# The attention's weighing of values as three fp32r products, its low parts on VectorE and GpSimd, with five places for x and a new order at the end of the attention

## What is computed

```
x = x + tanh(g_xattn) * (softmax(mask(q k^T / sqrt(512))) v Wo^T + bo)   # q, k, v: linear in layernorm(x), ctx, ctx
scores = layernorm(x) gate_w^T; probs = softmax(scores)                  # n, t, e
g, m = top_k(probs over the tokens, k = 2 * 2048 / 8)
h = gelu(x[m] w1[e]) w2[e]                                               # x here: layernorm(x)
x = x + tanh(g_ffn) * scatter_add(g * h at m)
```

## Time and profile before

| | us |
|---|---|
| median of 3 runs | 1527.88 (1527.38 to 1529.64) |
| the profiled execution | 1530.52 |
| its span, first to last instruction | 1528.8 |
| TensorE busy | 1490.4 (97%) |
| VectorE, ScalarE, GpSimd busy | 991.0, 737.8, 557.4 |
| attention: first weighing, last weighing ends | 56.65, 153.86 |

### The profile page before, as it was taken

The page is one execution under the profiler, slowest core; times in us unless marked ns, Lnnn a source line. Parts: engine busy times, 40 slices in busy tenths (PEclk is TensorE's granted clock), DMA queues, the critical chain, the costliest instruction groups (busy, mean ns, idle before and its releaser), DMA issues.

```text
span 1528.8 us, 20345 instructions
## 1 busy us (share of the span) xinstructions
PE 1490.4 (97%) x7329; PEld 1227.4 (80%) x7329; DVE 991.0 (65%) x1737; ACT 737.8 (48%) x1298; POOL 557.4 (36%) x527
## 2 busy tenths in 40 slices
PE   7988899999999999999999999999999999999997
PEld 7765677888888888888888888888888888888886
DVE  3678875568757675767567666766667665766543
ACT  2267543455445544454445444545445545554533
POOL 2253344635443244404432344314440444323311
PEclk9999999999999999999999999999999999999999
DMA  7285623624324433334324423342424332442133
GB/s 234 79 281 173 205 91 111 172 83 104 105 89 84 110 99 95 76 92 106 93 90 90 116 85 110 70 120 67 131 51 114 85 111 83 83 111 83 42 77 76
DMA packets 101386, 163.37 MB, mean 107 GB/s; under 512 B 7411, under 2 KB 45315, under 8 KB 101285
## 3 DMA queue, kind: packets, MB, share of 16 engines
q1 hardware_dynamic: 86672, 128.16, 26.7%
q0 software_dynamic: 14400, 33.56, 11.5%
q10 hardware_dynamic: 213, 0.34, 0.1%
HBM read 128.48 MB, written 33.55 MB: 106 GB/s over the span
## 4 chain that ended last, share of the span: by engine, by line
PE 91%; DVE 4%; DMA 2%; ACT 2%; issue 1%; POOL 1%; POOLq 0%; SPq 0%; DVEq 0%; ACTq 0%
PE bank L1511 43%; PE bank L1397 35%; PE bank L1373 5%; PE bank L1690 2%; PE bank L601 1%; PE bank L577 1%; PE bank L418 1%; DMA x_s<-in_x 1%; PE bank L566 1%; DVE x L902 1%; ACT xn L656 0%; DVE atleast L1070 0%; PE bank L412 0%; DMA raw_k<-in_L_xattn_Wk 0%; PE bank L1560 0%
## 5 line engine op out<-in xcount | busy, mean ns | idle before, releaser
L1511 PE MATMUL bank<-w2hl,hh 128*128 128x512 f32 x2024 | 628.4, 392 | 0.5 <-DVE hid_low L1489 0.5
L1397 PE MATMUL bank<-xo,whl 128*128 128x512 f32 x2352 | 541.6, 389 | 0.1
L1397 PEld LDWEIGHTS bank<-xo,whl 128*128 128x128 f32 x2352 | 441.3, 188 | 92.3 <-issue 0.4
L1511 PEld LDWEIGHTS bank<-w2hl,hh 128*128 128x128 f32 x2024 | 375.9, 188 | 75.6 <-DVE hid_low L1489 0.9
L1511 PE MATMUL bank<-w2hl,hid_low 128*128 128x512 f32 x1012 | 394.0, 389 | 0.0
L1511 PEld LDWEIGHTS bank<-w2hl,hid_low 128*128 128x128 f32 x1012 | 190.0, 188 | 39.6
L1637 POOL DMA_INDIRECT layer_out<-y,slot_row x64 | 104.3, 1629 | 295.6 <-ACT y L1550 280.3
L1356 DVE TENSOR_TENSOR w2hl<-raw,w2hl 128x512 fp32r<-128x512 f32 x215 | 150.5, 722 | 41.3 <-ACT w2hl L1351 41.3
L1325 POOL TENSOR_TENSOR whl<-raw,whl 128x512 fp32r<-128x512 f32 x56 | 81.3, 1451 | 258.3 <-ACT whl L1282 258.3
L1351 ACT ACTIVATE w2hl<-raw 128x512 fp32r<-128x512 f32 x228 | 136.5, 624 | 64.5 <-DMA raw<-in_L_ffn_w 43.3
L1330 POOL TENSOR_TENSOR whl<-wsum,whl 128x512 fp32r<-128x512 f32 x56 | 73.0, 1303 | 183.5 <-ACT whl L1303 183.5
(11 more groups left out here) (243 smaller groups left out, 1747.4 us busy)
## 6 DMA issues: line engine op xcount, KB each, us to landing
raw<-in_L_ffn_w SPq DMA_DIRECT2D x228, 256.0 KB, 2.7
raw<-in_L_ffn_w SPq DMA_DIRECT2D x72, 512.0 KB, 4.9
x_s<-in_x SPq DMA_DIRECT2D x8, 1024.0 KB, 9.6
layer_out<-x SPq DMA_DIRECT2D x8, 1024.0 KB, 10.1
xn_rows<-xn SPq DMA_DIRECT2D x8, 1024.0 KB, 5.2
raw_k<-in_L_xattn_Wk SPq DMA_DIRECT2D x1, 1024.0 KB, 6.5
raw_q<-in_L_xattn_Wq SPq DMA_DIRECT2D x1, 1024.0 KB, 8.7
raw_v<-in_L_xattn_Wv SPq DMA_DIRECT2D x1, 1024.0 KB, 11.1
```

The lines of the kernel that those rows point to most:

```text
L1397: last = pe.matmul(bk[:, :], whl[:, p % 2, part, 2 * w + k, :], xo[:, xpart, x, k, :], start=(not adds and k == 0 and part == HIGH and xpa ...
L1511: last = pe.matmul(Y_BANKS[c][:, :], high if hpart == HIGH else low[:, c * P:(c + 1) * P], w2hl[:, f % 4, part, :], start=(s == 0 and hpar ...
```

## The change

- All quads but the last are weighed by three fp32r products (`weigh_pe`). `vo` is split in high and low once, in prep: high copies by ScalarE (batch 0) and VectorE (batch 1) from PSUM ahead of the copies of before, low parts by GpSimd. The turned exponentials are split for each quad: ScalarE makes the high part from `eT` after its copy (`e_high`); the low part (`weights_low`) is made by VectorE in quads 0 to 3, between `router_in` and `weights_in`, and by GpSimd in quads 4 to 6, between the mask biases and the deviations.
- In quads 0 to 3 two of the x transposes go between the weighings.
- x has five places, two of them where raw_v and raw_o were; quads 3 and 4 are loaded in prep as these are turned, later ones when the quad five back is added. `square` and `weigh` read the same tiles there.
- Quad 3: only its first two tiles are squared by ScalarE; VectorE takes the other two with its statistics (`late_half`), after the softmax step of quad 4.
- Quad 6: `router_in` goes ahead of `values_dve`. Quad 7: ScalarE's copies of w1 go behind the exponentials and their copy.
- After the quads the tokens' low parts go ahead of the w1 halves (one of which stood between weighings) and of both last `logits_out`; the two w2 low parts go behind `choice_start_dve` of batch 1. ScalarE alternates tokens and squares.

The diff, without the new tensors' and semaphores' lines and `x_tile`, which picks a quad's place:

```diff
@@ -160,8 +161,10 @@
             raw_v, raw_o, wvT, woT = (outward.enter_context(nc.sbuf_tensor(n, [P, KD, D], F32))
                                       for n in ("raw_v", "raw_o", "wvT", "woT"))
         with ExitStack() as there:
-            there.enter_context(nc.sbuf_tensor("front", [P, 2, KD, CAP], F32R))
+            x_far = there.enter_context(nc.sbuf_tensor("x_far", [P, 2, Q, D], F32))
             spare = there.enter_context(nc.sbuf_tensor("spare", [P, 2, Q, D], BF16))
+            vo_split = there.enter_context(nc.sbuf_tensor("vo_split", [P, 2, D], F32R))
+            eT_split = there.enter_context(nc.sbuf_tensor("eT_split", [P, 2, Q * P], F32R))
         xp = overlay("xp", [P, B, 2, KD, CAP], F32R)
         hid1 = overlay("hid1", [P, KF, CAP], F32)
         hid1_low = keep("hid1_low", [P, KF, CAP], F32R)
@@ -527,6 +542,10 @@
                                                  gates[:, 0:1], ALU.add, ALU.mult)
                 elif name == "vo":
                     eng.wait_ge(consts, 3)
+                    if i == 0:
+                        eng.activation(vo_split[0:J, HIGH, :], bk[0:J, :], ACT.Copy).then_inc(vo_high, 1)
+                    else:
+                        eng.tensor_copy(vo_split_1[0:J, HIGH, :], bk[0:J, :]).then_inc(vo_high_1, 1)
                     last = copy(vo[0:J, i, :], bk[0:J, :])
                 elif name == "vg":
                     last = copy(vg[0:J, :, 0:E], bk[0:J, 0:B * E].rearrange("p (b e) -> p b e", b=B))
@@ -598,6 +619,19 @@
         def weigh_pe(pe, q, i):
             n = Q * q + i
             wait(pe, added, n - 1)
+            if q < SPLIT_QUADS:
+
+                if i == 0:
+                    pe.wait_ge(vo_low, q // QB + 1)
+                    pe.wait_ge(e_high, q + 1)
+                for epart, part in ((HIGH, HIGH), (HIGH, LOW), (LOW, HIGH)):
+                    if i == 0 and epart == LOW:
+                        pe.wait_ge(e_low, q + 1)
+                    last = pe.matmul(O_BANKS[n % 2][:, :], eT_split[0:J, epart, i * P:(i + 1) * P],
+                                     (vo_split, vo_split_1)[q // QB][0:J, part, :], start=(epart == HIGH and part == HIGH),
+                                     stop=(epart == LOW))
+                last.then_inc(weighed, 1)
+                return
             pe.matmul(O_BANKS[n % 2][:, :], eT[:, q % 2, i * P:(i + 1) * P], vo[:, q // QB, :],
                       start=True, stop=True).then_inc(weighed, 1)
@@ -630,11 +664,16 @@
                 for i in range(2):
                     weigh_pe(pe, q, i)
                 between(q, 1)
-                weigh_pe(pe, q, 2)
-                between(q, 2)
-                weigh_pe(pe, q, Q - 1)
-                between(q, 3)
-                for i in range(Q):
+                if q < QB:
+                    for i in range(2):
+                        turn_x(pe, q + 2, i)
+                        weigh_pe(pe, q, i + 2)
+                else:
+                    weigh_pe(pe, q, 2)
+                    between(q, 2)
+                    weigh_pe(pe, q, Q - 1)
+                    between(q, 3)
+                for i in range(2 if q < QB else 0, Q):
                     if q + 2 < NQ:
                         turn_x(pe, q + 2, i)
                     if i == 1:
@@ -647,6 +686,12 @@
             for c in range(NC):
                 tokens_pe(pe, 0, c)
+        def weights_low(eng, q):
+
+            eng.wait_ge(e_high, q + 1)
+            eng.tensor_tensor(eT_split[0:J, LOW, :], eT[0:J, q % 2, :], eT_split[0:J, HIGH, :].bitcast(F32),
+                              ALU.subtract).then_inc(e_low, 1)
+
         def rows_act(act, q, tiles):
             for i in tiles:
@@ -677,7 +722,7 @@
                     act.wait_ge(x1_mean, q - LATE + 2)
                 ins = act.activation(spare[:, 1, i, :], x1[:, q % 2, i, :], ACT.Square,
                                      bias=x1mean[:, q % 2, i:i + 1], accum_out=x1var[:, q % 2, i:i + 1])
-                if i == Q - 1:
+                if i == (Q // 2 if q == LATE else Q) - 1:
                     ins.then_inc(x1_squares, 1)
             def x_out(q, i):
@@ -700,25 +745,21 @@
                     act.wait_ge(weighed, Q * (q - 1))
                 act.wait_ge(consts, 3)
                 act.activation(eT[0:J, q % 2, :], turn_bank(("e", q, 0))[0:J, :], ACT.Copy).then_inc(turn_out, 1)
+                if q < SPLIT_QUADS:
+                    wait(act, weighed, Q * q)
+                    act.wait_ge(turn_out, turn_at["e", q, 0] + 1)
+                    act.activation(eT_split[0:J, HIGH, :], eT[0:J, q % 2, :], ACT.Copy).then_inc(e_high, 1)
             for q in range(2):
                 for i in range(Q):
                     x_out(q, i)
             prep_out(act, prep_act, True, 1)
             for q in range(NQ):
-                if q == NQ - 1:
-                    for p in range(2):
-                        w1_high_act(act, 0, 0, p)
-                elif q - 1 >= LATE:
+                if LATE <= q - 1 < NQ - 2:
                     for i in range(Q // 2):
                         square_x1(q - 1, i)
                 exps(q)
-                if q == CHOOSE_FROM:
-
-                    for i in range(Q // 2, Q):
-                        square_x1(q - 1, i)
-                    e_out(q)
-                elif CHOOSE_FROM < q < NQ - 1:
+                if CHOOSE_FROM < q < NQ - 1:
                     square_x1(q - 1, Q // 2)
                     e_out(q)
                     square_x1(q - 1, Q - 1)
@@ -727,6 +768,8 @@
                 if q == CHOOSE_FROM:
                     choice_act(act, 0)
                 if q == NQ - 1:
+                    for p in range(2):
+                        w1_high_act(act, 0, 0, p)
                     for f in range(2):
                         w2_high_act(act, 0, 0, f)
                     for i in range(Q):
@@ -742,11 +785,10 @@
             for i in range(2):
                 square_x1(NQ - 1, i)
-            first_tokens_act(act, 0)
-            for i in range(2, Q):
-                square_x1(NQ - 1, i)
-            for c in range(1, NC):
+            for c in range(NC):
                 first_tokens_act(act, c)
+                if c < 2:
+                    square_x1(NQ - 1, c + 2)
         def attention_pool(pool):
             own = Tally(pool_own)
@@ -771,7 +813,12 @@
                     own.mark(pool.tensor_scalar(nm[:, s, 0, :], mv[:, s, :, 1], EPS, None, ALU.add))
                     own.mark(pool.tensor_scalar(nm[:, s, 1, :], mv[:, s, :, 0], -1.0, None, ALU.mult))
                 else:
-                    own.mark(pool.tensor_scalar(nm[:, s, 0, :], x1var[:, s, :], 1.0 / D, EPS, ALU.mult, ALU.add))
+                    tiles = Q // 2 if q == LATE else Q
+                    own.mark(pool.tensor_scalar(nm[:, s, 0, 0:tiles], x1var[:, s, 0:tiles], 1.0 / D, EPS, ALU.mult,
+                                                ALU.add))
+                    if q == LATE:
+                        pool.wait_ge(late_stats, 1)
+                        own.mark(pool.tensor_scalar(nm[:, s, 0, tiles:Q], mv[:, s, tiles:Q, 1], EPS, None, ALU.add))
                 pool.wait_ge(pool_own, own.n)
                 pool.tensor_tensor(nm[:, s, 2, :], nm[:, s, 0, :], powers[:, :], ALU.pow).then_inc(deviated2, 1)
                 pool.wait_ge(deviated2, q + 1)
@@ -820,6 +867,16 @@
                 mask_biases(it + 1)
                 if it == 0:
                     first_deviations(1)
+                    pool.wait_ge(vo_high, 1)
+                    wait_evacuated(pool, step_at["vo", 0])
+                    pool.tensor_tensor(vo_split[0:J, LOW, :], vo[0:J, 0, :], vo_split[0:J, HIGH, :].bitcast(F32),
+                                       ALU.subtract).then_inc(vo_low, 1)
+                    pool.wait_ge(vo_high_1, 1)
+                    wait_evacuated(pool, step_at["vo", 1])
+                    pool.tensor_tensor(vo_split_1[0:J, LOW, :], vo[0:J, 1, :], vo_split_1[0:J, HIGH, :].bitcast(F32),
+                                       ALU.subtract).then_inc(vo_low, 1)
+                if QB <= it < SPLIT_QUADS:
+                    weights_low(pool, it)
                 q = it - 1
                 if q >= 0:
                     deviations(q)
@@ -918,6 +975,17 @@
                     last = dve.bn_aggr(mv2[:, q % 2, i, :], st2[:, i, :])
                     own.mark(last) if i < Q - 1 else last.then_inc(x1_stats, 1)
+            def late_half():
+
+                dve.wait_ge(x1_stats, LATE)
+                dve.wait_ge(deviated2, LATE - 1)
+                for i in range(Q // 2, Q):
+                    own.mark(dve.bn_stats(st2[:, i, :], x1[:, LATE % 2, i, :]))
+                dve.wait_ge(dve_own, own.n)
+                for i in range(Q // 2, Q):
+                    last = dve.bn_aggr(mv2[:, LATE % 2, i, :], st2[:, i, :])
+                    own.mark(last) if i < Q - 1 else last.then_inc(late_stats, 1)
+
             def mean_out(q, tiles=slice(0, Q)):
                 dve.wait_ge(added, Q * q + tiles.stop)
```

(33 more changed lines are left out.)

22 lines of the change are left out of this document (17 added, 5 removed).

## The result

The changed kernel takes 1532.53 us (median of 21 runs, 1529.31 to 1535.05), the one before 1527.76 (21 runs, 1526.27 to 1530.41). The ratio is 1.0026, 95% interval 1.0021 to 1.0032: **slower by 4 to 5 us** (4.0 by the ratio, 4.8 by the medians), where +1.0 was forecast. The execution that was profiled took 1531.46, with a span of 1529.7: 0.9 more than the span before. So this trace holds only a part of the difference, and one more reason than its rows show is needed.

A forecast was written before the change was run, and what follows sets the result against it. TensorE bounds only the stretch to 102 us, VectorE's instruction order the rest. Up to quad 6's second addition -0.5 + 0.4 + 1.0 + 1.0 = +1.9, quad 7 -1.1, tail +0.2: +1.0, 1528.9 us; range 1523.5 to 1532.5.

The forecast's parts named there:

- the 1.0 taken: Quads 5 and 6: GpSimd's subtraction stretches a VectorE instruction, 1.0 us lost each time, ends 0 and 1.3.
- the -1.1 of the sum: Quad 7: router copy ahead of values and exponential ahead of the w1 copies save 1.1 us together.
- near 168: Tail: the first output product was expected near 168 us as a sign that the forecast is right.
- Rival 3: Third product waits so long that quads get no shorter; the 1.9 are missing, 1530.8; chance inside the forecast's 0.48.
- the 2.5 that I took: Quads 1 to 3: VectorE becomes the bound, so 2.5 us arrive of the 4.9 that TensorE is rid of.
- the 9.8 of the sum: Quad 1's softmax period: 4.9 + 0.62 + 0.55 + 3.72 = 9.8 us, 11.0 before the change.
- The lead: Start of quad 4: its softmax begins 1.9 us earlier, ends 1.2 and 2.5.
- the 1.4: Start of the choice: 1.4 of the 1.9 us gained by then are given back, leaving 0.5 earlier.
- the chain through `e_high`: From quad 4's exponential through transposes, two copies and GpSimd's subtraction to quad 3's deviations, done at 101.4 us.
- 0.4 for it: Quad 4, beside the choice: a lower clock lengthens one count of 16 products by 0.4 us, ends 0 and 1.5.
- Rival 2: Clock falls once more in quad 5; transposes and scores 1.8 longer, counts 1.4: +2.5, 1531.4; chance 0.20.
- the 6.41 that I kept: Quad 7: its unsplit weighings were taken to last 6.41 us at the lower clock, as before the change.

The follow-up runs named there:

- small products everywhere: Changed kernel plus small unread TensorE products in idle time, in front and in quads 4 to 6: 1527.92 us, +0.6 by ratio against the kernel before.
- front only: Changed kernel split only in quads 0 to 3, plus small unread TensorE products in front and fewer behind: 1524.35 us, -4.1 by ratio against the kernel before.

## Where the prediction held and where it failed

**Held.** VectorE as the bound of the front; the third product waiting for the low part, in quads 2 to 4; 0.6 lost at the start (61.94 against 61.39; from the first x transposes on, which began 0.14 later, it is 0.4); GpSimd's low part ahead of the deviations; one stretched instruction a quad, +0.93 and +0.85 for the 1.0 taken. Here the rule cited from the Trainium skill (SBUF — State Buffer, Who interferes with whom) and the trace agree, and the run with the low parts on VectorE shows the cause. Quad 7: from +3.7 at quad 6's second addition to +2.6 at quad 7's weighings, the -1.1 of the sum. The tail: tokens 1.1 sooner, for 0.8; first output product at 168.41 for "near 168". Rival 3 fell: quads 1 to 3 got shorter by 1.4 in all, if by less than the 2.5 that I took.

**Failed: VectorE gapless in the front.** The periods were summed from VectorE's own work and TensorE's; the softmax step has a third releaser, GpSimd's `first_deviations`, behind two normed rows. It starts when `moments` ends. GpSimd's first small step, 0.23 us before the change, takes 0.68 now, beside VectorE's new subtraction (66.81 and 66.72). For quad 1 the 9.8 of the sum and this wait of 0.58 give 10.4, and 10.43 was measured. The lead was 0.9 and not 1.9, below its own lower end of 1.2. What the sum credits to the three products comes without them: by the new order and the places alone quads 1 to 3 last 10.1, 10.7 and 10.8 us in fp32. The forecast had no case of that. It also took too much off TensorE, 0.29 a weighing: a weighing with the four transposes behind it takes 1.15 us (80.18 to 81.33) against 1.30 in the run without the split, so 0.15 less. That changed nothing, since VectorE was the bound.

**Failed: the start of the choice**, forecast 0.5 sooner, measured 0.9 later. The mechanism was right. 1.0 of the 1.4 is the lead that wasn't there; the chain through `e_high` took 0.4 more than its links.

**Failed: the clock**, which is the main one. The sum had 0.4 for it, in quad 4 only. Rival 2 described a fall in quad 5 and had 0.20; I set against it that no fall stands there before. It took place (0.50 at 126:128, 0.80 at 132:134 where TensorE makes quad 6's scores), and the 1531.4 of that rival is the nearest of the forecast's values to what was measured. No case at all had a fall in front, though the same paragraph that called VectorE the bound said that TensorE would need 9.6 us of each 10 to 11: a stage whose bound moves off TensorE leaves TensorE idle in each quad. The run with small products everywhere shows 3.4 to 4.6 us, which is the distance between the changed kernel and the one before. With them the kernel stands at +0.6 (-0.8 to 1.8), and the forecast without its 0.4 for the clock would be +0.6; what the products cost of themselves is in the measured value, and not known for this kernel.

**Why the profiled execution looked right.** Its difference of +0.9 is the forecast's +1.0, by errors that cancel. +1.8 at quad 6's second addition (choice and clock) stand against -0.9 from quad 7's weighings, 5.54 us for the 6.41 that I kept, -0.3 from the tokens, and -0.8 behind them: from the first hidden product to the first output product 0.7 more than before and not 1.2, and 0.5 made good afterwards and not 0.2. That the range held is luck of this kind too: the forecast's band (1526 to 1530.9) missed, 1532.53 lies at the very end of the range of 1532.5, and the chance given to a slower kernel was 0.24.

The profiled execution also had no fall in front. Its mean clock, 0.989, is the highest of the 21; the others have 0.984 to 0.988. That the difference of two profiled executions "goes to the median" was a step of the sum too, and it failed: the changed kernel's runs spread over 5.7 us, and their mean clocks differ from 0.984 to 0.989: falls come in some executions and not in others. Not all spread is that. In prep, before 20 us, the same 32 products (L418, L428 in the changed kernel) take 4.44 us in five of the fourteen profiled executions and 6.2 to 6.8 in the other nine, of kernels with and without the change, at a granted clock of 1.00. That moves all that follows by about 2 us and is a likely part of the spread of 4.1 us before the change. Both main profiles have the longer form, so their difference is free of it. Its cause stays open.

**The account.** No split -5 (order, places, squares). Split in front: +1 VectorE, +2 clock. Split in quads 4 to 6: 6 us, of which 4.7 stay with the small products (those everywhere less front only). To these belong the choice's later opening (2.5: 40.9 against 38.3) and the two stretched instructions (1.8). The rest, 1.4 by the times and 1.6 by the rows, is the clock: 0.5 in quad 4, 0.3 in quad 5, 0.75 in quad 6. Each of these parts carries an uncertainty of 1 to 2 us where it comes from times, and of one execution where it comes from rows.
